# Image recurrence: centring one turn behind the adding, input product one turn behind the normalising

## The reference

```python
    h = h + _L0_ffn_ref(_layernorm(h, axis=-1), ...)      # y_tok = ybuf[idx, pos_g] * (prb * kept)[:, None]
    h = h + _L1_attn_ref(_layernorm(h, axis=-1), L1_attn_W_ih, L1_attn_W_hh, L1_attn_b_ih, L1_attn_b_hh)
    # _L1_attn_ref: the first axis, the 16 images, is the time of the recurrence
    xp = jnp.einsum('tbi,hi->tbh', x_in, W_ih) + b_ih + b_hh
    def step(h, xp_t):
        h_new = jnp.tanh(xp_t + h @ W_hh.T)
        return (h_new, h_new)
    _, hiddens = jax.lax.scan(step, h0, xp)
```

## Time and profile before

| | us |
|---|---|
| median of 3 runs | 4280.12 |
| lowest and highest | 4279.72, 4288.03 |
| the profiled execution's own time | 4307.09 |
| its span | 4305.3 |

### The profile page before, as it was taken

The page is one execution under the profiler, slowest core; times in us unless marked ns, Lnnn a source line. Parts: engine busy times, 40 slices in busy tenths (PEclk is TensorE's granted clock), DMA queues, the critical chain, the costliest instruction groups (busy, mean ns, idle before and its releaser), DMA issues. The chain is left out here.

```text
span 4305.3 us, 68585 instructions
## 1 busy us (share of the span) xinstructions
PE 3164.1 (73%) x25552; PEld 1810.4 (42%) x25552; DVE 2515.9 (58%) x3049; ACT 2136.0 (50%) x3049; POOL 2570.3 (60%) x1541
## 2 busy tenths in 40 slices
PE   8999996999999950000079936666676799999997
PEld 6777774555555530000034412222222355555555
DVE  7888886888888852000035513333335777777773
ACT  5667665777777720000034425555564445555542
POOL 7777773887878825777700055555523666666661
PEclk9999998999999965555589968777877999999998
DMA  1111111122222120111033323333321121221221
GB/s 40 41 40 41 36 40 62 58 69 74 86 70 74 53 74 31 40 45 40 14 94 108 112 57 95 96 94 95 87 86 61 32 57 52 60 62 49 58 57 42
DMA packets 252195, 267.20 MB, mean 62 GB/s; under 512 B 86568, under 2 KB 168140, under 8 KB 251805
## 3 DMA queue, kind: packets, MB, share of 16 engines
q1 hardware_dynamic: 215566, 228.51, 17.0%
q0 software_dynamic: 25600, 21.10, 2.8%
q10 hardware_dynamic: 10704, 13.20, 0.9%
HBM read 127.66 MB, written 140.20 MB: 62 GB/s over the span
## 5 line engine op out<-in xcount | busy, mean ns | idle before, releaser
L1512 POOL DMA_INDIRECT D_row<-yb,D_idx x400 | 381.4, 954 | 645.7 <-DMA D_prob<-keepp 348.0
L2169 POOL TENSOR_TENSOR E_w<-E_w,E_rs 128x1024 f32<-128x1024 f32 x200 | 380.3, 1902 | 314.5 <-DVE E_rs L2092 314.5
L1241 POOL DMA_INDIRECT xb<-R_row,R_si x400 | 388.9, 972 | 212.3 <-issue 121.5
L1314 PE MATMUL X_px<-X_ident,X_xs 128*128 128x128 f32 x256 | 42.9, 291 | 559.4 <-DMA X_xs<-xb 559.4
L180 POOL TENSOR_TENSOR A_kmask<-A_ksb,A_pack_a 128x3584 f32<-128x3584 f32 x56 | 356.4, 6364 | 152.8 <-ACT A_ksb L327 152.8
L1373 ACT ACTIVATE X_hm<-X_ph,X_b 128x512 f32<-128x512 f32 x128 | 88.0, 688 | 595.4 <-PE X_ph L1326 595.4
L1388 DVE COPY X_xt<-X_px 128x512 f32<-128x512 f32 x64 | 43.6, 681 | 530.9 <-PE X_px L1314 530.9
L2163 POOL TENSOR_TENSOR E_hs<-E_w 128x512 f32<-128x512 f32 x200 | 254.8, 1274 | 100.3 <-ACT E_w L2042 100.3
L1314 PEld LDWEIGHTS X_px<-X_ident,X_xs 128*128 128x128 f32 x256 | 27.5, 143 | 608.1 <-DMA X_b<-in_e_b 559.6
L2076 DVE TENSOR_REDUCE E_mx<-E_lg 128x16 f32<-128x1024 f32 x200 | 237.4, 1187 | 70.4 <-PE E_lg L1881 69.6
L2042 ACT ACTIVATE E_w<-E_w 128x1024 f32<-128x1024 f32 x200 | 211.4, 1057 | 134.2 <-DVE E_w L2084 131.8
(11 more groups left out here) (298 smaller groups left out, 8444.4 us busy)
## 6 DMA issues: line engine op xcount, KB each, us to landing
xb<-B_blank SPq DMA_DIRECT2D x64, 256.0 KB, 4.0
X_xs<-xb SPq DMA_DIRECT2D x64, 256.0 KB, 2.8
yb<-X_ys SPq DMA_DIRECT2D x64, 256.0 KB, 2.0
B_x<-h SPq DMA_DIRECT2D x25, 512.0 KB, 4.3
h<-B_hh SPq DMA_DIRECT2D x25, 512.0 KB, 3.7
y<-B_yt SPq DMA_DIRECT2D x25, 512.0 KB, 2.6
R_row<-y SPq DMA_DIRECT2D x25, 512.0 KB, 3.4
A_xg<-in_xw SPq DMA_DIRECT2D x56, 224.0 KB
```

Source lines behind the costliest of these rows:

```text
L1241: pool.indirect_dma_start(out=xb, out_offset=bass.IndirectOffsetOnAxis(ap=si[:, B * c + b:B * c + b + 1], axis=0), in_=row[c % U][:, D * r ...
L1512: pool.indirect_dma_start(out=row[n % LR][:, k, b], out_offset=None, in_=yb, in_offset=bass.IndirectOffsetOnAxis(ap=idx[:, c, i:i + 1], ax ...
L2169: TT(w3, w3, bc(rs[g % 3][:].unsqueeze(2), [128, 2 * SH, G]), ALU.mult).then_inc(w_done, 1)
```

## The change

No instruction is added or taken away; steps move within the loops. Centring, square and variance of the input go one turn back; log, root and normed_in from one turn behind the adding to two; inputs and first_hidden from one to three; the tanhs, second_hidden and add_hidden from two to four; the output's centring, square and variance from three to five, its normalising from four to six, turn_y and tokens from five to seven. The loops are two turns longer. center_in is issued ahead of turn_rows, and variance ahead of variance_out. x has five buffers instead of three, y two instead of one.

```diff
-        x = [m.sb(f"x{u}", [128, W]) for u in range(3)]
-        sq, r, y, sq2, r2 = (m.sb(n, [128, W]) for n in ("sq", "r", "y", "sq2", "r2"))
+        x = [m.sb(f"x{u}", [128, W]) for u in range(5)]
+        sq, r, sq2, r2 = (m.sb(n, [128, W]) for n in ("sq", "r", "sq2", "r2"))
+        y = [m.sb(f"y{u}", [128, W]) for u in range(2)]
...
-                for t in range(N + 6):
+                for t in range(N + 8):
                     at(load, t + 2)
-                    at(keep_k, t - 5)
-                    at(keep_y, t - 4)
-                    at(keep_h, t - 2)
+                    at(keep_k, t - 7)
+                    at(keep_y, t - 6)
+                    at(keep_h, t - 4)
...
-                for t in range(N + 5):
-                    at(turn_y, t - 5)
+                for t in range(N + 7):
+                    at(turn_y, t - 7)
+                    at(center_in, t - 1)
                     at(turn_rows, t)
-                    at(center_in, t)
-                    at(inputs, t - 1)
-                    at(center_out, t - 3)
-                    at(first_hidden, t - 1)
-                    at(second_hidden, t - 2)
-                    at(variance_out, t - 3)
-                    at(variance, t)
+                    at(inputs, t - 3)
+                    at(center_out, t - 5)
+                    at(first_hidden, t - 3)
+                    at(second_hidden, t - 4)
+                    at(variance, t - 1)
+                    at(variance_out, t - 5)
...
-                for t in range(N + 4):
+                for t in range(N + 6):
                     nc.scalar.preload_act_table_set(LN_EXP)
-                    at(log_in, t - 1)
-                    at(log_out, t - 4)
-                    at(root_in, t - 1)
-                    at(root_out, t - 4)
+                    at(log_in, t - 2)
+                    at(log_out, t - 6)
+                    at(root_in, t - 2)
+                    at(root_out, t - 6)
                     nc.scalar.preload_act_table_set(TANH)
-                    at(first_tanh, t - 2)
-                    at(square_in, t)
-                    at(square_out, t - 3)
-                    at(second_tanh, t - 2)
+                    at(first_tanh, t - 4)
+                    at(square_in, t - 1)
+                    at(square_out, t - 5)
+                    at(second_tanh, t - 4)
...
-                    after(dve, cen_done, n - 2)
-                    after(dve, h_done, n - 2)
+                    after(dve, cen_done, n - 4)
+                    after(dve, h_done, n - 4)
...
-                    after(dve, ih_done, n)
+                    after(dve, ih_done, n - 1)
...
-                for t in range(N + 5):
-                    at(tokens, t - 5)
+                for t in range(N + 7):
+                    at(tokens, t - 7)
                     at(weigh, t)
                     at(add_experts, t)
-                    at(normed_in, t - 1)
-                    at(normed_out, t - 4)
-                    at(add_hidden, t - 2)
+                    at(normed_in, t - 2)
+                    at(normed_out, t - 6)
+                    at(add_hidden, t - 4)
```

More of the change, by code:

```diff
@@ L1524, in turn_rows @@
                     after(pe, x_done, n)
-                    after(pe, yk_done, min(n - 4, N))
+                    after(pe, yk_done, min(n - 6, N))
                     for k in range(len(tiles(n))):
@@ L1532, in center_in @@
                     after(pe, y_done, n - 1)
-                    mm(pc[n % 2][:, 0:wide(n)], center[:], x[n % 3][:, 0:wide(n)], start=True, stop=True).then_inc(cen_done, 1)
+                    mm(pc[n % 2][:, 0:wide(n)], center[:], x[n % 5][:, 0:wide(n)], start=True, stop=True).then_inc(cen_done, 1)
                 def variance(n):
@@ L1542, in inputs @@
                     after(pe, tb_done, n - 1)
-                    mm(px[n % 2][:, 0:wide(n)], wih[:], y[:, 0:wide(n)], start=True, stop=n < J,
+                    mm(px[n % 2][:, 0:wide(n)], wih[:], y[n % 2][:, 0:wide(n)], start=True, stop=n < J,
                        skip_group_check=True).then_inc(ih_done, 1)
@@ L1568, in turn_y @@
                     pe.wait_ge(yo_done, n + 1)
-                    after(pe, x_done, min(n + 5, N))
+                    after(pe, x_done, min(n + 7, N))
                     for k in range(len(tiles(n))):
@@ L1663, in add_experts @@
                     dve.wait_ge(h_in[n % LH], 16 * (n // LH + 1))
-                    after(dve, cen_done, n - 2)
-                    after(dve, h_done, n - 2)
-                    TT(x[n % 3][:, 0:wide(n)], pt[:, 0:wide(n)], hx[n % LH][:, 0:wide(n)], ALU.add).then_inc(x_done, 1)
+                    after(dve, cen_done, n - 4)
+                    after(dve, h_done, n - 4)
+                    TT(x[n % 5][:, 0:wide(n)], pt[:, 0:wide(n)], hx[n % LH][:, 0:wide(n)], ALU.add).then_inc(x_done, 1)
                 def normed_in(n):
@@ L1670, in normed_in @@
                     dve.wait_ge(cen_done, n + 1)
-                    after(dve, ih_done, n)
-                    TT(y[:, 0:wide(n)], pc[n % 2][:, 0:wide(n)], r[:, 0:wide(n)], ALU.mult).then_inc(y_done, 1)
+                    after(dve, ih_done, n - 1)
+                    TT(y[n % 2][:, 0:wide(n)], pc[n % 2][:, 0:wide(n)], r[:, 0:wide(n)], ALU.mult).then_inc(y_done, 1)
                 def add_hidden(n):
@@ L1679, in add_hidden @@
                     after(dve, h_out[n % 2], 16 * (n // 2))
-                    TT(h[n % 2][:, 0:wide(n)], x[n % 3][:, 0:wide(n)], hid[n // J % 2][:, cols(n)],
+                    TT(h[n % 2][:, 0:wide(n)], x[n % 5][:, 0:wide(n)], hid[n // J % 2][:, cols(n)],
                        ALU.add).then_inc(h_done, 1)
```

## The result

| | us |
|---|---|
| before, median of 22 runs beside it | 4286.37 (4265.53 to 4306.40) |
| after, median of 22 runs | 4296.56 (4281.79 to 4303.69) |
| ratio | 1.0023, interval 1.0012 to 1.0034 |
| profiled execution after, its span | 4296.76, 4294.9 |

The change made the kernel 10 us slower, where 32 us faster was forecast. The time lies in the forecast's range (4130 to 4312 us), on the wrong side of no change. The profiled execution of after is itself 10 us shorter than that of before, of which the stage has 0.6 us (748.3 us from its first instruction to its last before, 747.7 after); the rest lies in other stages. So the profiles can tell where the forecast gain went, and not where the last 0.2% came from.

A forecast was written before the change was run, and what follows sets the result against it. The bound was taken to be a loop of back-to-back gathers, late TensorE signals and POOL pauses. Seven pairs at 6.3 us less gave 44, minus 12 for two deeper turns: 32 us off, 4248 us; range 4130 to 4312.

The forecast's parts named there:

- U: Length of an undisturbed turn, weighing to weighing: 8.3 us forecast, taken between 6.9 and 9.1.
- the joining of nearly every second batch: On POOL, the second batch of eight gathers always follows the first unbroken, turns being shorter than a 10 us batch.
- the signal waited for: In a disturbed double turn, the late TensorE signal becomes second_hidden's or variance_out's instead of center_out's.
- POOL's pauses: Sign in the trace: after 16 gathers without a gap, POOL pauses 5 us instead of 8.3.
- The two turns more at the end: End of the stage: the pipeline, two turns deeper, costs 12 us there.
- R: Time from the end of 16 unbroken gathers to the weighing after next: 7.3 us before, 4.0 forecast.
- 3 x (20.6 + R) + U: A pair of images as three double turns and one short turn: 82.1 us, 6.3 less per pair.
- the full clock oftener: TensorE, with the same work in less time, runs at full clock more; variance_out takes 1.1 us there, 2.1 at half.
- the first pair: Start of the stage, dominated by gathers that run ahead; left out of the seven pairs counted as gaining.
- Rival (c): Slower: every second batch of gathers joins while R stays at 7.3; 92.0 us a pair, total 4317; chance 0.22.
- Late signals come with gathers: Unbroken gathers on POOL make TensorE's signals reach ScalarE late, as in a 7.1 us wait before square_out; taken as real.
- Rival (a): Gathers bound the stage, late signals don't matter: 63.7 us a pair, 161 off, 4119; chance 0.18 including times toward the forecast.

The follow-up runs named there:

- e6: Changed kernel in which POOL, before each batch of gathers, waits until the last batch's rows have landed: 4252.16 us, 1.0351 of the kernel before.
- e14: Changed kernel with half the gathers (from the fifth block on only the first image's rows): 4061.57 us, 0.9880 of the kernel before.
- e8: Changed kernel with TensorE's old order (turn_rows ahead of center_in, variance_out ahead of variance): 4117.34 us, 1.0016 of the kernel before.
- e12: Changed kernel with TensorE's old order, run once more on another chip: 4128.86 us, 1.0013 of the kernel before.
- e13: Kernel before with half the gathers (from the fifth block on only the first image's rows): 4101.60 us, 0.9970 of the kernel before.
- e2: Changed kernel with the gathers taken out after the first four blocks: 4061.43 us, 0.9466 of the kernel before.
- e1: Kernel before with the gathers taken out after the first four blocks: 4103.97 us, 0.9553 of the kernel before.

## Why the prediction was wrong

- **Right:** the undisturbed turn (U, 8.3 forecast, 7.3 to 8.6 seen), the joining of nearly every second batch (three stood 1.3 to 1.7 us off after the change, nine stood 0.6 to 1.5 off before, though the forecast had none left), and that the signal waited for would be a later one (second_hidden's). POOL's pauses in the six inner pairs were 3.7 to 9.9 us and are 3.6 to 6.0 now (5 forecast), but for one in each pair (8 to 14 us), mostly in the slow turn:

```profile
2831.74 0.95 POOL L1513 DMA_INDIRECT D_row<-yb,D_idx  x1 [10.86 <-DVE D_scaled L1659]
```

- The two turns more at the end cost 14.2 us, where 12 was forecast.
- **Mis-sized:** R. Forecast 4.0, measured 4.6 in the turn shown, with half a microsecond more until the gathers end (21.1, not 20.6). The double turns of that pair are 25.7, 25.8 and 24.4 us instead of 24.6: 2.1 of the pair's miss.
- **The step that failed:** "3 x (20.6 + R) + U", with the short turn behind the batch of two gathers counted as undisturbed. It is the turn behind a pause. I took TensorE to have "the full clock oftener" in the denser turns; instead its queue, now emptied before the stall, left it idle in the stall, and that turn runs at half clock: 13.1 for 8.3, 4.8 of the miss. Together 6.9, and 82.1 + 6.9 is the 89.0 measured in this pair; the mean of the six is 87.6, so 5.5 over the forecast. That an idle stretch ahead of this turn goes with the half clock, whatever made TensorE idle, e6 shows (4.3 us, no late signal, 13.1 us again). It is not the whole cause: behind 7.5 us of idleness the turn at 2792.01 took 8.4 us, and with no idle stretch at all (e14) the third turn took 8.6 us in three of the inner pairs and 11.6 to 11.9 at granted clock 0.71 in the other three. What decides whether the clock falls in this turn stays open.
- **Also missed:** the first pair, which I left at no gain, gave 2.5 us, and the last 8.1 where I had 6.3.
- **Rival (c)** named the right side and the wrong cause: R did not stay at 7.3, and 4317 is 20 us above the median. Its clause, center_in and variance put ahead where they stand on the path at half clock, does show in the slow turn (1.9 us for variance). e8 and e12, which put them back, fell on chips without late signals: the total was the same, though in e8 the third turn kept the full clock. What the order costs beside late signals stays open.
- **The premise.** "Late signals come with gathers" is true of the program on some chips only. Rival (a), which I priced at 4119 us, is what chips C, D and E show: 4112, for both kernels alike. There I would have been wrong in another way: I measured (a)'s gain from a before of 4280, while on such a chip before is at 4112 too, and the change is worth nothing. By the rule of the Trainium skill (SBUF — State Buffer, section SBUF: two separate sides) engine ports and DMA ports are apart and TensorE waits for nobody. The runs on C, D and E agree. On B and F gathers did delay what ScalarE got from TensorE; the rule speaks of ports and not of signals, and whether a port had to do with it no run shows.

So the 40 us that the shifts are worth (e14 against e13, e2 against e1) are lost in two ways: on one kind of chip the changed kernel meets POOL's 62.5 us to a pair, on the other it gives back, in one half-clock turn to a pair and in the longer end, what its double turns win.

What stays open: why a chip has late signals, what the residual 0.2% is, and what makes the clock fall in the third turn. No chip changed its kind while runs were taken on it.

## What to carry to other kernels

Deepening a software pipeline pays only where the turn's own chain is the bound; halving the work of the engine beside it (here the gathers) shows in one run what it would be worth. A turn behind a stall is not an undisturbed one: look up TensorE's granted clock turn by turn before counting it at full speed. And where an argument rests on odd behaviour in one trace, run the kernel before on another chip first.

## What was unexpected of the hardware

- The same kernel takes 4277 to 4294 us on some chips and 4111 to 4113 on others, while its gathers have the same pace (0.95 to 0.98 us, 0.30 apart). Nearly the whole difference lies in this stage (748 and 565 us, 183 of the 191 between the two spans).
- With gathers back to back, ScalarE's waits for late signals of TensorE reached 10.2 us on the first kind of chip; with the same bytes moved by SyncE's transfers there were none, and the time was 4032 to 4048 us on either kind.
- 1.5 us between batches gave 1.1% on one such chip and 2.2% on another.
- The same turn of the same pair ran at granted clock 1.00 or 0.71 in one trace (e14: 8.6 or some 11.9 us, in alternate pairs), though the two turns before it took 7.9 and 8.2 us in either case and TensorE had no idle stretch of over 2 us in them.
